# Zero stores and down-weight repacking issued by SyncE instead of ScalarE, and 60 instead of 52 maxima ahead of the expert tiles

## The reference, cut to what matters

```
xn = layernorm(x)
s  = attention(xn)                  # layer 0: 32 heads of width 8, 8 key/value heads, causal softmax
g  = silu(moe(xn))                  # layer 0: 32 experts, width 96, the best 4 for each token
x  = x + s * g
xn = layernorm(x)
s  = gated_delta_rule_block(xn)     # layer 1: 32 value heads, state 128 x 128
g  = silu(moe1(xn))                 # layer 1: 8 experts, width 176, the best 2
x  = x + s * g
```

## Time and profile before

| what | us |
|---|---|
| median of 3 runs | 2314.36 (2313.28 to 2314.37) |
| the profiled execution | 2313.63 |
| its span in the profile | 2311.6 |
| TensorE busy over the span | 2015.2 (87%) |
| VectorE busy over the span | 1538.9 (67%) |
| ScalarE busy over the span | 982.5 (43%) |
| GpSimd busy over the span | 758.4 (33%) |
| mean granted clock of TensorE, share of full | 0.962 |

### The profile page before, as it was taken

The page is one execution under the profiler, slowest core; times in us unless marked ns, Lnnn a source line. Parts: engine busy times, 40 slices in busy tenths (PEclk is TensorE's granted clock), DMA queues, the critical chain, the costliest instruction groups (busy, mean ns, idle before and its releaser), DMA issues.

```text
span 2311.6 us, 39665 instructions
## 1 busy us (share of the span) xinstructions
PE 2015.2 (87%) x13026; PEld 1516.7 (66%) x13066; DVE 1538.9 (67%) x2459; ACT 982.5 (43%) x2529; POOL 758.4 (33%) x685
## 2 busy tenths in 40 slices
PE   4578888884588599999999999999999999999996
PEld 2257643334344387878778778787787787877875
DVE  3968841124555577777777777777777777777775
ACT  1012247761010345545445355454454544545544
POOL 4630011102000415336154262361542524615332
PEclk8889989996799799999999999999999999999998
DMA  7446630000011000000000000000000000000001
GB/s 264 147 153 197 196 103 27 18 1 23 23 32 44 25 33 28 14 32 27 9 27 14 32 27 14 23 20 25 27 14 32 27 13 24 18 27 27 14 23 37
DMA packets 72034, 107.37 MB, mean 46 GB/s; under 512 B 22918, under 2 KB 54934, under 8 KB 68790
## 3 DMA queue, kind: packets, MB, share of 16 engines
q1 hardware_dynamic: 64446, 86.60, 12.0%
q10 hardware_dynamic: 4478, 11.88, 1.4%
q0 software_dynamic: 3072, 8.39, 1.1%
HBM read 81.48 MB, written 28.52 MB: 48 GB/s over the span
## 4 chain that ended last, share of the span: by engine, by line
PE 48%; DVE 13%; ACT 3%; issue 3%; POOL 0%; DMA 0%; DVEq 0%; ACTq 0%; POOLq 0%
PE ps L1430 6%; PE ps L1558 5%; PE ps L1550 5%; PE ps L1468 4%; PE ps L1478 3%; DVE P L1961 3%; DVE P_term L1958 3%; DVE conv L1882 3%; PE ps L1615 3%; PE ps L1493 2%; PE ps L1604 2%; PE ps L1564 2%; PE ps L1504 2%; PE ps L1617 2%; PE ps L1591 2%
## 5 line engine op out<-in xcount | busy, mean ns | idle before, releaser
L1882 DVE SCALAR_TENSOR_TENSOR conv<-raw,tap_st,conv 128x1024 f32<-128x1024 f32 x204 | 299.9, 1470 | 3.8
L1430 PE MATMUL ps<-xnT,w_conv_st 128*128 128x512 f32 x544 | 250.4, 599 | 4.4 <-DMA w_conv_st<-in_w_conv 4.4
L1862 POOL TENSOR_TENSOR o<-o,silu_z 128x256 f32<-128x256 f32 x128 | 138.3, 1080 | 255.7 <-DVE silu_z L1902 141.7
L824 DVE TENSOR_REDUCE m_part<-ps 128x1 f32<-128x640 f32 (+7 forms) x176 | 175.1, 1026 | 49.1 <-PE ps L675 32.7
L1756 POOL TENSOR_TENSOR gmask_Q<-upto,g 128x2048 f32<-128x2048 f32 x17 | 61.4, 3610 | 433.7 <-PE ps L1571 433.6
L1635 ACT COPY raw<-ps 128x512 f32<-128x512 f32 x136 | 80.7, 594 | 271.3 <-PE ps L1430 271.3
L990 ACT ACTIVATE probs<-ps 128x1024 f32<-128x1024 f32 (+7 forms) x256 | 146.0, 660 | 44.5 <-PE ps L940 24.1
L1430 PEld LDWEIGHTS ps<-xnT,w_conv_st 128*128 128x128 f32 x544 | 97.7, 191 | 97.2 <-issue 88.6
L1842 POOL TENSOR_TENSOR kq_decayed<-conv,decay_rows 128x1024 f32<-128x1024 f32 x64 | 158.3, 2504 | 0.0
L1478 PE MATMUL ps<-w_z_st,xnT 128*128 128x256 f32 x512 | 148.8, 393 | 0.0
L1468 PE MATMUL ps<-w_out_st,xn_nat 128*128 128x256 f32 x544 | 126.2, 386 | 0.7
(11 more groups left out here) (340 smaller groups left out, 4741.7 us busy)
## 6 DMA issues: line engine op xcount, KB each, us to landing
decay_rows<-scratch_egc SPq DMA_DIRECT2D x17, 1024.0 KB, 4.7
w_conv_st<-in_w_conv SPq DMA_DIRECT2D x17, 512.0 KB, 3.3
scratch_slots_x<-yacc ACTq DMA_DIRECT2D x8, 1024.0 KB, 10.2
slot_rows<-scratch_slots_x SPq DMA_DIRECT2D x16, 512.0 KB, 5.0
scratch_slots_y<-slot_outputs SPq DMA_DIRECT2D x16, 512.0 KB, 3.8
w_gate_up<-in_gu SPq DMA_DIRECT2D x8, 768.0 KB, 8.0
w_gate_up<-in_gu SPq DMA_DIRECT2D x32, 192.0 KB, 3.1
w_out_st<-in_w_out SPq DMA_DIRECT2D x17, 256.0 KB, 2.6
```

The lines of the kernel that those rows point to most:

```text
L824: dve.tensor_reduce(dst, src, AX.X, ALU.max).then_inc(s_max, 1)
L1430: mm = pe.matmul(ps[:, 6 + n % 2, :], wc[:, k, (n // 2) * P:(n // 2 + 1) * P], m.xnT[:, k, (n % 2) * HALF:(n % 2 + 1) * HALF], start=k == ...
L1862: g.tensor_tensor(oc, oc, zs[:, c, :], ALU.mult).then_inc(s_oz, 1)
L1882: op = dve.scalar_tensor_tensor(out=cv[:, t, :], in0=raw[:, t, at:at + T], scalar=tap[:, t, at:at + 1], in1=cv[:, t, :], op0=ALU.mult, op1 ...
```

## The change

The eight stores of zeros move from ScalarE to SyncE, behind SyncE's four input loads; SyncE waits there for GpSimd to have made the zeros. The eight repacking DMAs move to SyncE as well, behind the load of stack 0, at the end of its stream in the first stage. ScalarE's waits for x and for the weights go with them. In the second stage SyncE loads stacks 1 and 2 before it waits for the repacked weights (`s_rows`) and loads the weights of steps 0 and 1; stacks 3 and 4 stay behind them. `FIRST_OP` goes from 52 to 60, and `first_op(g)` becomes 60 + 7g + (g + 3) // 4: steps 0, 4, 8 and 12 keep their eight ops, steps 3, 7, 11 and 15 their seven, and steps 1, 2, 5, 6, 9, 10, 13 and 14 go from eight to seven. The number of ops is the same, 176.

```
@@ stage_inputs, sync @@
             sp.dma_start(m.w_o[:], w_o.rearrange("(k p) n -> p k n", p=P)).then_inc(in_wo, 16)
+            sp.wait_ge(s_clear, 1)
+            for i in range(SLOTS // T):
+                sp.dma_start(m.slots_x[T * i:T * (i + 1), :].rearrange("(p a) d -> p (a d)", p=P),
+                             m.yacc[:].rearrange("p c d -> p (c d)")).then_inc(m.s_zeroed, 16)
...
             load_stacks(sp, m, 0)
+            for i in range(E0 // G0):
+                sp.dma_start(m.down_rows[G0 * i:G0 * (i + 1)].rearrange("g f d -> (g f) d").rearrange("(t p) d -> p t d", p=P),
+                             down0[i].rearrange("p (t d) -> p t d", d=D)).then_inc(m.s_rows, 16)
             sp.wait_ge(in_wo, 16)
@@ stage_inputs, scalar @@
-            act.wait_ge(s_clear, 1)
-            act.wait_ge(in_x, 16)
-            act.wait_ge(in_w, 32)
-            for i in range(SLOTS // T):
-                act.dma_start(m.slots_x[T * i:T * (i + 1), :].rearrange("(p a) d -> p (a d)", p=P),
...
-            for i in range(E0 // G0):
-                act.dma_start(m.down_rows[G0 * i:G0 * (i + 1)].rearrange("g f d -> (g f) d").rearrange("(t p) d -> p t d", p=P),
...
             for k in range(KT):
                 act.wait_ge(s_tr, k + 1)
@@ the order of ops @@
-FIRST_OP = 52
+FIRST_OP = 60
-    return FIRST_OP + g * 8 - g // 4
+    return FIRST_OP + g * 7 + (g + 3) // 4
@@ stage_maxima_and_moe0, sync @@
+            load_stacks(sp, m, 1)
+            load_stacks(sp, m, 2)
             sp.wait_ge(m.s_rows, 16 * (E0 // G0))
             for g in range(2):
                 load_weights(g, g)
-            for group in range(1, 5):
-                if group == 4:
-                    sp.wait_ge(s_sc, 1)
-                load_stacks(sp, m, group)
+            load_stacks(sp, m, 3)
+            sp.wait_ge(s_sc, 1)
+            load_stacks(sp, m, 4)
```

More of the change, by code:

```diff
@@ L467, in _ @@
         def _(act):
-            act.wait_ge(s_clear, 1)
-            act.wait_ge(in_x, 16)
-            act.wait_ge(in_w, 32)
-            for i in range(SLOTS // T):
-                act.dma_start(m.slots_x[T * i:T * (i + 1), :].rearrange("(p a) d -> p (a d)", p=P),
-                              m.yacc[:].rearrange("p c d -> p (c d)")).then_inc(m.s_zeroed, 16)
-            for i in range(E0 // G0):
-                act.dma_start(m.down_rows[G0 * i:G0 * (i + 1)].rearrange("g f d -> (g f) d").rearrange("(t p) d -> p t d", p=P),
-                              down0[i].rearrange("p (t d) -> p t d", d=D)).then_inc(m.s_rows, 16)
             for k in range(KT):
```

## The result

| | kernel before | changed kernel |
|---|---|---|
| median of the timed runs, us | 2313.28 | 2304.72 |
| lowest and highest of 7, us | 2310.39, 2320.86 | 2303.62, 2305.66 |
| span of the profiled execution, us | 2311.6 | 2302.7 |

The ratio is 0.9959, with a 95% interval of 0.9947 to 0.9971: faster by 9.5 us, 6.7 to 12.3. The forecast of 2298.5 had the sign, and the time lies in its range; the forecast gain was 15.6 us.

A forecast was written before the change was run, and what follows sets the result against it. The first stage was taken to be bound by ScalarE's DMA issuing, the later steps partly by a ring. 11.0 + 0 + 4.6 = 15.6 us off 2313.63 gave 2298.0, with 0.7 for the median 2298.5; range 2291 to 2306.

The forecast's parts named there:

- Part 1: First stage: ScalarE, freed of DMA issues, copies at once after the transposes, so TensorE's projections start 12.4 us earlier.
- up to 2 us of the clock: First 4 us of the projections: at the higher clock up to 2 us more may come off; none was counted.
- Part 2: First stage: SyncE issues zeros at no cost and repacking in 8.8 us, ending last; the stage ends 11.0 us earlier.
- Rival A: First stage: SyncE's repacking takes as long as on ScalarE, so the stage ends 3 us early; 2306 us, chance 0.13.
- rival E: First stage: the move does not matter, the copy would have waited for something else; 2309 us, chance 0.03.
- rival D: First stage: zeros in x's queue delay x, so normalization starts 21 to 23 us late; 2320 us, chance 0.04.
- Part 3: Second stage: SyncE loads stacks 1 and 2 before waiting for the repacked rows; value zero either way.
- Part 4: Start of the tiles: 60 operations ahead delay the first turn 2.5 us, the higher clock saves 2.5; net zero.
- Part 5: The 16 steps: eight operations fewer, four worth nothing and four their TensorE spacing; 4.6 us together, bounds 0 to 8.9.
- the ring: Steps' second bound: down, output copy, store, row issue, landing, turn, gate_up, next down; removed operations may only lengthen row waits.
- stack 7's wait of 0.7 us: Steps: SyncE's 0.7 us wait for op 66 ahead of stack 7 goes, as op 66 is now in step 0.
- Rival B: The steps: the ring takes all of the gain from fewer operations; 2302 or 2303 us, chance 0.18.

The follow-up runs named there:

- moves alone: The changed kernel with the old order of operations (FIRST_OP 52, old first_op), only the DMA issues moved and stacks first: 2298.66 us, 0.9945 of the kernel before.
- order alone: The kernel before with only the new order of operations (FIRST_OP 60, new first_op), ScalarE still issuing: 2314.18 us, ratio 1.0008.
- early rows: The changed kernel with SyncE issuing the next step's rows between gate_up's and down's weights: 2317.67 us (0.9911) with 60 ahead, 2310.37 (0.9882) with 52.
- third series: Runs on one chip of the unaltered changed kernel (2333.82 us) and variants issuing rows earlier, against the kernel before at 2338.43 us.
- second series: Runs on another chip of the unaltered changed kernel (2334.97 us), stack 7 behind weights, zeros behind x, and four edits together, against the kernel before at 2342.80 us.

## Why the prediction was right, and where it failed

**Part 1** (ScalarE freed, 12.4 us). Right in the mechanism and nearly in size: the projections start 11.5 us earlier, since x's later landing takes 0.9. The up to 2 us of the clock, which I saw and took none of, came in the projections (9.09 to 7.11), but the stage's end moved by 12.14, so 0.6 of them are left there.

**Part 2** (SyncE loaded, stage 11.0 us earlier). The repacking was priced at 8.8 and took 6.12, below my lower bound of 7.3. I had taken the cheapest of the issues behind the zeros, 0.91, for the floor; in the new place their median is 0.62, and the eleven other traces with them there have 5.4 to 6.4 us for the eight. Rival A fell by that, and rival E by the moves alone. So SyncE did not become the last, and the stage's end moved by 12.14 us. The zeros, costed at nothing, cost 0.9 at x in this pair of profiles (0.6 in the other series): rival D in the small, where I had argued from a small DMA behind a large one that those behind do not hurt those in front.

**Part 3** (stacks 1 and 2 first, zero). No wait for a stack stands in TensorE's waits: as forecast.

**Part 4** (60 ahead, net zero). Right on the chip of the measurement: no gap, clock 1.00, and at the first tanh 1.2 us better than the 12.14 of the stage's end alone. The first interval takes the 1.2 back (below), so at the second tanh (142.04 and 129.87) the lead is 12.17: net zero, as forecast. The condition that carried it, GpSimd's chain being last, was the one to name: on two other chips it doesn't hold, and on the one of them where both orders ran the same edit costs 5.4 us.

**Part 5** (eight operations fewer, 4.6 us) **is the step that failed.** It gave -4.1 us in the profiles, and nothing in the time of the order alone (1.0008); its own lower bound was zero. I had named the ring, and then judged by the turns of the old trace that four of eight operations stood in steps which it did not hold, and that the ring would hand back the other four as longer waits. The intervals between the tanhs say where it went otherwise:

| intervals | before | changed | order alone |
|---|---|---|---|
| first (eight operations in both orders) | 9.20 | 10.36 | 10.36 |
| third and fourth (turns of steps 3 and 4) | 26.68 | 29.71 | 27.46 |
| seventh and eighth (turns 7 and 8) | 22.71 | 21.40 | 21.05 |
| eleventh and twelfth (the split, turns 11 and 12) | 23.48 | 25.60 | 23.34 |
| fourteenth and fifteenth (turns 14 and 15) | 23.66 | 22.16 | 23.69 |
| the other six | 66.52 | 67.04 | 66.20 |

Of the three turns which I had found without a wait, 8 and 15 still have none, and the changed kernel gained 1.3 and 1.5 us in the pairs of intervals that hold them, 1.0 and 0.8 of it by waits at turns 7 and 14 that became shorter or went. The third, 12, now waits 1.33 us. Of the turns that had waited behind a removed operation, 3 and 4 wait longer (3.74 to 4.43, 0.85 to 1.34), but 7 and 11 shorter (1.46 to 0.45, 0.99 to 0.35): the ring does not hand an operation back turn by turn, as my sum had it. The first interval costs 1.2 us in every profile with the new order (10.36 or 10.37 in eleven, 9.20 or 9.21 in the three with the old): a step of as many operations, but of others, the first two of a group among them. I had no term for that. The loss at the eleventh and twelfth is absent in the order alone and in the changed kernel's second profile (23.32), so it is not the order's. At the third and fourth the three profiles of the changed kernel have 29.71, 29.85 and 27.86, the moves alone 27.15 and the order alone 27.46: 1 to 3 us of loss with both, which no run takes apart.

Two terms more were missing. I priced an operation by its time and not by what it covers: the one that was removed was the cover of ScalarE's 0.7 us copy, 8.1 us uncovered instead of 4.2. And I let stack 7's wait of 0.7 us go as a gain and did not count the nine issues of that stack, some 4 us on SyncE, which stand in the ring ahead of the rows of step 3 in either order. TensorE waited 3.7 us there before, with a granted clock of 0.57 from 156 to 160 us behind it, and 4.4 now, with 0.50 and 0.72 in the two rows from 144 to 152; taking the issues away gave 4.8 us.

**The sum.** 12.1 + 1.2 - 4.1 = 9.2 at the attention's start, against 11.0 + 0 + 4.6 forecast. The stage was under-forecast by 1.1 and part 4 by 1.2; part 5 was over-forecast by 8.7 in this pair of profiles and by 4.6 if the order alone, with nothing gained, is taken for it. Rival B, the ring takes all of part 5, was the nearest of the cases (2302 to 2303), with a chance of 0.18.

**How firm this is.** That the moves carry the gain, and that the place of the rows on SyncE bounds the steps, is shown by separate runs with clear intervals. That the order of 60 does harm in the changed kernel, and is not merely useless, rests on one profile pair (176.27 and 172.25), while other profiles of the unaltered changed kernel have 171.9 and 180.2, and no timed run shows it: the order alone is 0.9997 to 1.0018. With early rows, on the chip of the third series, the harm is shown (7.3 us, 2.7 to 11.9), with the first turn 5.4 later in the profiles.

## What to carry to other kernels

Before work is taken out of a loop step, find the ring that closes around it and break that first; here the loads of rows, which stood on the issuing engine behind a wait for an old buffer, a store and once nine other loads, were worth 16 us when they were put ahead of them, and the shorter steps nothing. Ask what the removed operation covered, and which operations take its place in the other steps. An engine's issuing time in front of a compute instruction that others wait for is worth moving; its price in the new place is not the old one (6.12 us for 16.62), and only a run there gives it.

## What the hardware showed unexpectedly

Eight issues of the same 384 KB transfers took 16.62 us on ScalarE behind zeros and 6.12 us on SyncE behind a small load. The eight zeros took 8.37 us on ScalarE, 5.07 on SyncE from 3.22 us, with x not yet landed, and 8.28 on SyncE from 7.87 us, behind x. So the time of an issue isn't fixed, and a fuller queue isn't always the slower one; for the repackings the engine changed with the place, and no run tells the two apart.

Zeros issued in the same queue behind x delayed x's landing by 0.9 us (5.7 to 6.6), and putting them behind its landing gave 0.6 back in the other series (6.5 to 5.9): in these traces, standing ahead in the queue did not wholly protect x.

The granted clock fell to 0.50 behind a single wait of 4.4 us (144 to 148 us), and to 0.56 and 0.58 from 164 to 172 behind one of 5.1 in the second series. In the changed kernel it also fell behind the wait of only 1.83 us at the split (0.70 from 240 to 244 us).

One program did 58 maxima on one chip and 40 on another in the same 56 us, with the difference in idle time before TensorE's operations.
